# Choosing other work when fewer than two PSUM banks are free, in an attention and FFN kernel ordered by a planner

## Time and profile before

| what | value |
|---|---|
| median of three runs | 811.6 us |
| the profiled execution | 810.76 us |
| its span, first to last instruction | 808.9 us |
| TensorE (PE) busy | 793.1 us, 98% |
| VectorE (DVE) busy | 596.6 us, 74% |
| ScalarE (ACT) busy | 410.8 us, 51% |
| GpSimd (POOL) busy | 336.2 us, 42% |
| mean granted TensorE clock | 1.000 |

### The profile page before, as it was taken

The page is one execution under the profiler, slowest core; times in us unless marked ns, Lnnn a source line. Parts: engine busy times, 40 slices in busy tenths (PEclk is TensorE's granted clock), DMA queues, the critical chain, the costliest instruction groups (busy, mean ns, idle before and its releaser), DMA issues.

```text
span 808.9 us, 14257 instructions
## 1 busy us (share of the span) xinstructions
PE 793.1 (98%) x4987; PEld 470.3 (58%) x4987; DVE 596.6 (74%) x1817; ACT 410.8 (51%) x862; POOL 336.2 (42%) x347
## 2 busy tenths in 40 slices
PE   7999999999999999999999999999999999999998
PEld 3676454544456645656656655565666556465675
DVE  6869888698988757686796856769487777769313
ACT  4523545564655645555464554636365463556462
POOL 4494249346451175559142228728702013122120
PEclk9999999999999999999999999999999999999999
DMA  7962615232517362241343516143060544310021
GB/s 265 281 172 79 173 54 170 94 93 94 170 55 173 105 175 88 95 124 73 84 141 88 139 53 186 64 133 119 2 207 17 130 97 111 88 36 20 3 78 53
DMA packets 66358, 88.60 MB, mean 110 GB/s; under 512 B 7360, under 2 KB 34880, under 8 KB 66288
## 3 DMA queue, kind: packets, MB, share of 16 engines
q1 hardware_dynamic: 66288, 87.70, 37.2%
HBM read 49.71 MB, written 37.98 MB: 108 GB/s over the span
## 4 chain that ended last, share of the span: by engine, by line
PE 91%; ACT 5%; DVE 2%; issue 1%; DMA 1%; SPq 0%; ACTq 0%; DVEq 0%
PE o_bank L1254 16%; PE banks L1175 15%; PE banks L1147 14%; PE banks L1163 14%; PE banks L1236 14%; PE banks L1121 7%; ACT probs L1044 4%; PE banks L1130 4%; PE banks L1202 3%; PE banks L1240 2%; DVE banks L1455 1%; PE banks L1111 1%; DMA bqk_sb<-in_bk 1%; DVE part_max L1452 0%; PE banks L1152 0%
## 5 line engine op out<-in xcount | busy, mean ns | idle before, releaser
L1044 ACT ACTIVATE probs<-banks 128x512 f32<-128x512 f32 (+1 forms) x608 | 309.5, 583 | 268.5 <-PE banks L1240 142.9
L1236 PE MATMUL banks<-q_st,k_st 99*128 99x512 bf16 (+3 forms) x768 | 209.1, 327 | 4.9 <-ACT probs L1044 1.4
L1175 PE MATMUL banks<-k_st,q_st 96*128 96x512 bf16 (+3 forms) x768 | 210.9, 327 | 0.4 <-DVE row_max L1455 0.3
L1452 DVE TENSOR_REDUCE part_max<-banks 128x1 f32<-128x512 f32 x256 | 159.4, 677 | 8.8 <-PE banks L1175 8.5
L1455 DVE CUSTOM_DVE_ANT_0 banks<-banks,tri,part_max 128x512 f32<-128x512 f32 (+3 forms) x256 | 128.2, 554 | 49.3 <-PE banks L1175 49.2
L1455 DVE CUSTOM_DVE_ANT_0 banks<-banks,tri 128x512 f32<-128x512 f32 (+3 forms) x256 | 118.9, 515 | 29.5 <-PE banks L1175 29.0
L1147 PE MATMUL banks<-xnT,w_sb 128*128 128x256 f32 x512 | 134.0, 385 | 0.6 <-ACT probs L1044 0.3
L1254 PE MATMUL o_bank<-probs,v_sb 128*17 128x512 f32 (+3 forms) x1536 | 133.2, 487 | 0.1
L903 POOL TENSOR_TENSOR hT<-hT,gates 128x512 f32<-128x512 f32 x48 | 55.5, 1158 | 160.4 <-ACT hT L1030 139.9
L1163 PE MATMUL banks<-w_sb,hT 128*128 128x256 f32 x512 | 120.8, 381 | 0.0
L1175 PEld LDWEIGHTS banks<-k_st,q_st 96*128 96x128 bf16 x768 | 71.8, 97 | 75.2 <-issue 18.2
(11 more groups left out here) (103 smaller groups left out, 753.2 us busy)
## 6 DMA issues: line engine op xcount, KB each, us to landing
term_scratch<-pieces SPq DMA_DIRECT2D x84, 256.0 KB, 2.9
q_st<-term_scratch SPq DMA_DIRECT2D x16, 768.0 KB, 5.9
k_st<-term_scratch SPq DMA_DIRECT2D x16, 768.0 KB, 8.5
y_scratch<-o_norm SPq DMA_DIRECT2D x31, 256.0 KB, 2.4
gates<-gate_scratch SPq DMA_DIRECT2D x24, 256.0 KB, 6.3
acc<-in_x SPq DMA_DIRECT2D x8, 512.0 KB, 3.8
rope_sb<-y_scratch SPq DMA_DIRECT2D x15, 256.0 KB
out<-acc SPq DMA_DIRECT2D x7, 512.0 KB, 2.9
```

The source lines that it names most:

```text
L1044: nc.scalar.activation(probs[:, h:h + shared(k), PROBS_AT[u]:PROBS_AT[u] + w], bank, ACT.Exp, scale=SCALE).then_inc(s_out, 1)
L1175: nc.tensor.matmul(bank[:, 0:w], q_st[0:KROWS, at, h, i * P:(i + 1) * P], k_st[0:KROWS, at, h, c * HALF:c * HALF + w], start=True, stop=Tr ...
L1236: last = nc.tensor.matmul(bank[:, i], k_st[0:SROWS, at, h + i, j * P:(j + 1) * P], q_st[0:SROWS, at, h + i, q0:q0 + w], start=(i == 0), st ...
L1452: ins = nc.vector.tensor_reduce(part_max[:, h, at:at + 1], bank[:, 0:w], AX.X, ALU.max)
```

## The change

Two edits, both in the planner. GATES goes from 20000 to 40000 columns. And between choices 2 and 3 of the list comes a new one: when `may_work` holds, fewer than two banks are free by the planner's clock, and the works done are below the share plus SPARE, a work is taken. Nothing is added to or taken from what each engine computes.

```
-GATED, GATES = 500, 20000
+GATED, GATES = 500, 40000
...
+    def room():
+        return sum(at <= clock for at in free)
...
                 elif may_work and done + cost(works[0]) / 2 <= share - SPARE:
                     if not wide and wide_max_ready():
                         do_max()
                     done += do_work(works)
+                elif may_work and room() < 2 and done < share + SPARE:
+                    done += do_work(works)
                 elif max_ready():
                     do_max()
```

## The result

The changed kernel takes 804.4 us (median of six, 803.9 to 805.0) where the kernel before, on the same chip, takes 811.6 us (six runs, 810.8 to 813.1): a ratio of 0.9915, 95% interval 0.9904 to 0.9926, or 7.2 us less. The forecast was 807.3 us with 801.5 to 813.5, and faster.

The account below looks back on a forecast made before the run. The prediction took TensorE to bound the kernel, with 26.5 us of bank stalls. Its terms, -6.6 + 1.3 + 0.5 + 0.5 = -4.3 us, took 810.76 us to 806.5, or 807.3 us as a median; range 801.5 to 813.5 us.

Parts of the forecast that it names:

- TensorE bounds, and its bank stalls are what can be won: TensorE, busy 98% of the span, sets the time; 26.5 us of its start delays are waits for banks.
- Head of the groups: Scores of k = 0 and 1: works placed there remove 60% of 11.0 us of bank stalls, -6.6 us.
- The rest of the group: Units from k = 2 on, with 15.5 us of stalls: works done early are missing there, +1.3 us net.
- Late rows: A group's last maxima, behind works, delay a few rows for the second half's scores: +0.5 us, bounds 0 and +9.
- Unready inputs: Works moved earlier on TensorE, chiefly a second part of ffn, meet inputs not ready: +0.5 us, bounds 0 and +3.
- GATES, 0 us alone: GpSimd's order of gates and splits: raising GATES without the new choice changes the time by 0 us.
- As cover, up to 8 us: GpSimd: with the new choice, GATES 40000 keeps a delayed split from queuing behind a waiting gate, up to 8 us.
- theory 2 of e1: Split behind a waiting gate on GpSimd: rows have 20 us to spare, nothing is urgent, so 804.4 us within 1.6.
- Rival A: Stalls only move from a group's head to k = 4 to 9: 811.6 us within 1.6 us, chance 0.21.
- Rival B: Maxima fall behind, rows come late at k = 4 of twelve groups: 815.7 us; chance 0.18 with other losses.
- Rival C: Larger gain, 90% of head stalls and a quarter of the others: -12.8 us, 798.8 us, chance 0.13.
- Sum: All terms over the whole kernel: -6.6 + 1.3 + 0.5 + 0.5 = -4.3 us.

Follow-up runs that it names:

- e11: The kernel before with 6 banks instead of 7 in planner and program: 838.0 us, ratio 1.0329 to the kernel before.
- e1: The changed kernel with GATES back at 20000, so the new choice alone: 843.0 us, ratio 1.0391 to the kernel before.
- e7: The changed kernel, with xnT of a later batch held until 8000 columns after the planner's book has its tokens normalised: 802.1 us, ratio 0.9891 to the kernel before.
- e5: The changed kernel with the new choice only for units k = 0 to 5 of each group: 810.8 us, ratio 0.9995 to the kernel before.
- e2: The changed kernel with the new choice only for units k = 0 and 1 of each group: 809.7 us, ratio 0.9984 to the kernel before.

## Why the prediction was right, and where it was not

- *TensorE bounds, and its bank stalls are what can be won*: right. The span fell by what the delays fell, and e11 shows the stalls follow the number of banks.
- *Head of the groups, -6.6 us*: the stalls there fell by 5.8 us, near it. Works were to stand between the first four scores of groups 1 to 12. They do in eight of them; in groups 1 and 5 they stand ahead of the run of pv instead, and maxima between the scores.
- *The rest of the group, +1.3 us net*: this term was mis-sized, in sign too. Stalls there fell by 3.4 us. In a group's later units the condition puts works at short moments better than the even share did. There was more to reach there than the prediction saw: of the 225 places, 128 were said to lie in k = 0 to 3, but the old planner, run again with these places counted, has 75 there and 150 later.
- *Late rows, +0.5 us*: nothing came of it. The first score of a second half never lost more than 0.12 us.
- *Unready inputs, +0.5 us*: mis-sized, other delays grew by 2.4 us. The prediction looked for works that come earlier. Where it cost, the inputs came later: VectorE's steps for the tokens of batch 1 and for a bank of pv ended 5 to 6 us later than before. The trace of before had xnT of batch 1 only 3.8 to 8.6 us after its tokens, and this was not priced.
- *GATES, 0 us alone*: as the planner's output shows. *As cover, up to 8 us*: this was far too little, 39 us (e1 against the changed kernel). The step that failed held the distance at 14.1 us and the loss at one wait; it was 27 us, came in three batches, had TensorE behind it through maxT, and cost clock on top. The 20 us that the rows have to spare (theory 2 of e1) did not help, as TensorE waits for the split itself and not for the rows.
- *Rival A, the stalls only move*: refuted by the 9.2 us that went. The Trainium skill (Perfetto Trace Analysis, Optimization Strategy) names too little SBUF or PSUM as a possible cause of consistent bubbles; e11 bears that out, and yet order alone won a third of them. *Rival B*: no part of it. *Rival C*: its 90% and its quarter were 53% and 22%.
- *Sum*: -5.8 - 3.4 + 2.4 = -6.8 us where -4.3 was forecast. That it is no further off is partly luck: the rest of the group came out 4.7 us better than forecast and the inputs 1.9 us worse.

Not settled: why the planner's order has VectorE's steps in batch 0 later with the new choice, and so which part of the choice runs into a late pv. Of these waits only the one for xn was taken away (e7). What decides whether a pause of 1.5 us lowers the clock is open too.

## What to carry to other kernels

When one engine is busy 98% of the time, read its starts against its columns: the columns made 734.7 of 793.1 us "busy", so 58 us, 7% of this kernel, were hidden there. Filler work is worth most where a shared buffer is about to run out, and is wasted when it is merely early; the condition on free banks was worth 20 us against the same choice without it. A planner that moves work must know every input of what it moves: one transfer thought 8 us away that took 27 cost more than five times what the new order won, and one unlisted input (xn) cost a fourth of the gain.

## What the runs showed of the hardware

After TensorE had stood still for 10.7 us in e1, its granted clock was 0.53 in the next 6 us, and 1.00 again behind them; scores and maxima of 512 columns started 0.43 us apart there instead of 0.22 us. The Trainium skill (TensorE: Matmul & The Clock Gate, What's actually happening) has it that the slow clock is the default state and that activity releases it; the trace agrees.

Much shorter pauses can have the same effect. Behind an idle 1.46 us in e5, and behind idle times of 1.74, 0.61 and 0.21 us close together in e2, the clock was at 0.51 and 0.50 in the stretches shown. The pause of e5 so cost about twice its length, 1.6 us by itself and 1.6 us in the items behind it. Yet in the profiled execution of the changed kernel, whose mean is 1.000, idle times of 1.34 and 1.52 us at 102 and 112 us did not lower it. No run here shows what sets them apart.

How far away a small transfer is depended on what stood ahead of it in the issuing engine's order. The mask's way from VectorE's read to the first gate took 14 us before and 27 us after, while the loads of gates took 5 to 8 us from issue to landing in both; what differs is when they were issued: the mask went out at once after the read before and 9.5 us after it in the changed kernel, and the loads 6.9 and 10.3 us after that.
